# Attention of an image block: exact scores from fp32 operands in two row tiles instead of a three-part bf16 split

## What is computed

```python
qkv = jnp.einsum('bnc,oc->bno', xt, qkv_w)            # xt: (16, 1024, 192)
q, k, v = ...                                          # each (16, 6 heads, 1024, 32)
attn = jnp.einsum('bhnd,bhmd->bhnm', q, k) * SCALE
attn = jax.nn.softmax(attn, axis=-1)
out = jnp.einsum('bhnm,bhmd->bhnd', attn, v)
out = jnp.einsum('bnc,oc->bno', out, proj_w) + proj_b
```

## Time and profile before

| | us |
|---|---|
| median of 3 runs | 14572.99 (14550.2 to 14592.92) |
| the profiled execution | 14591.93 |
| its span | 14590.1 |

### The profile page before, as it was taken

The page is one execution under the profiler, slowest core; times in us unless marked ns, Lnnn a source line. Parts: engine busy times, 40 slices in busy tenths (PEclk is TensorE's granted clock), DMA queues, the critical chain, the costliest instruction groups (busy, mean ns, idle before and its releaser), DMA issues. The chain is left out here.

```text
span 14590.1 us, 88624 instructions
## 1 busy us (share of the span) xinstructions
PE 8678.6 (59%) x26672; PEld 2793.6 (19%) x26816; DVE 9257.5 (63%) x8214; ACT 4330.1 (30%) x4371; POOL 6262.8 (43%) x2937
## 2 busy tenths in 40 slices
PE   6474674746648466484664846648466384663846
PEld 1121221212212122121221312113122131221312
DVE  4756747567485674856748566575665756657566
ACT  2323233232322323223232232322323223232232
POOL 2715417154171541715417154261642716427164
PEclk8676766767667676676766767767676676766767
DMA  3505125051240512405124051340513405134051
GB/s 81 125 16 137 46 73 125 16 142 41 79 120 16 144 39 80 119 16 144 39 79 120 16 147 36 86 112 16 150 35 83 113 16 150 36 84 113 16 150 36
DMA packets 364229, 1164.38 MB, mean 80 GB/s; under 512 B 61487, under 2 KB 63039, under 8 KB 363599
## 3 DMA queue, kind: packets, MB, share of 16 engines
q1 hardware_dynamic: 358363, 1155.62, 31.0%
q10 hardware_dynamic: 3988, 1.01, 0.1%
q0 software_dynamic: 1248, 0.64, 0.0%
HBM read 959.86 MB, written 121.63 MB: 74 GB/s over the span
## 5 line engine op out<-in xcount | busy, mean ns | idle before, releaser
L796 PE MATMUL ps<-arena,sel_y 128*32 128x512 f32 x6144 | 2200.3, 882 | 4138.9 <-POOL arena L1037 4138.9
L1037 POOL TENSOR_TENSOR arena<-arena 128x1024 f32<-128x1024 f32 x1536 | 3798.8, 2474 | 635.2 <-DVE arena L986 597.6
L986 DVE TENSOR_TENSOR_SCAN arena<-ps,arena 128x1024 f32<-128x1024 f32 x1536 | 3514.6, 2290 | 717.2 <-POOL arena L1027 682.1
L902 ACT ACTIVATE ps<-arena,v_na 128x1024 f32<-128x1024 f32 x1536 | 1713.5, 1118 | 4085.7 <-DVE arena L986 3476.6
L796 PEld LDWEIGHTS ps<-arena,sel_y 128*32 128x32 f32 x6144 | 471.6, 150 | 5876.7 <-POOL arena L1037 3739.4
L617 DVE TENSOR_REDUCE arena<-ps 128x1 bf16<-128x1024 f32 x768 | 933.8, 1223 | 1015.6 <-PE ps L480 1015.0
L1027 POOL TENSOR_TENSOR arena<-arena 128x1024 f32<-128x1024 f32 x512 | 1201.3, 2346 | 468.7 <-DMA arena<-scan_dtu 468.7
L1019 POOL TENSOR_TENSOR arena<-arena,XN 128x1024 f32<-128x1024 f32 x32 | 75.2, 2350 | 2871.1 <-DVE arena L931 2871.1
L980 DVE TENSOR_TENSOR arena<-arena,ps 128x1024 f32<-128x1024 f32 x768 | 919.3, 1197 | 534.9 <-DMA arena<-scan_dtu 534.9
L597 ACT ACTIVATE arena<-ps 128x1024 f32<-128x1024 f32 x768 | 744.2, 1021 | 1056.4 <-PE ps L532 1056.4
L532 PE MATMUL ps<-arena 65*128 65x512 bf16 (+1 forms) x2928 | 759.3, 397 | 62.6 <-ACT arena L597 26.2
(11 more groups left out here) (213 smaller groups left out, 12246.7 us busy)
## 6 DMA issues: line engine op xcount, KB each, us to landing
arena<-scan_dt SPq DMA_DIRECT2D x768, 512.0 KB, 4.6
arena<-scan_dtu SPq DMA_DIRECT2D x768, 512.0 KB, 4.6
arena<-scan_bc SPq DMA_DIRECT2D x256, 512.0 KB, 6.3
arena<-arena SPq DMA_DIRECT2D x1152, 64.0 KB, 2.0
scan_dt<-arena SPq DMA_DIRECT2D x64, 512.0 KB, 9.8
scan_dtu<-arena SPq DMA_DIRECT2D x64, 512.0 KB, 7.6
scan_dt<-arena SPq DMA_DIRECT2D x64, 256.0 KB, 11.0
scan_dtu<-arena SPq DMA_DIRECT2D x64, 256.0 KB, 11.2
```

The source lines that it names most:

```text
L796: mm = nc.tensor.matmul(ps[3][32 * q:32 * q + 32, HALF * h:HALF * h + HALF], sel_y[:, r, :], hc[i % NHC][:, HALF * h:HALF * h + HALF], sta ...
L902: nc.scalar.activation(ps[1 + i % 2][:], dtr[:, i // 2 % RING, :], ACT.Exp, scale=v_na[:, at:at + 1]).then_inc(m_da, 1)
L986: nc.vector.tensor_tensor_scan(hs[:, i % 2, o], ps[1 + i % 2][:, o], bu[:, i % 2, o], 0.0, ALU.mult, ALU.add).then_inc(m_h, 1)
L1037: pool.tensor_tensor(hc[i % NHC], hs[:, i % 2, :], Cb[:, 2 * (k // 2) + f, :], ALU.mult).then_inc(m_hc, 1)
```

## The change

Queries and keys of a head stay fp32. Head h lies in tile h // 2 at row 64 * (h % 2), 32 rows, of `QQ` and `KK`; the weights `w_q` and `w_k` are laid out with zeros between (22 more weight loads before the image loop, in 32-column pieces). The row behind the 32 is 1 in the keys (a bias vector `v_one` on the copy from PSUM) and the negated maximum in the queries. The exact scores are one fp32 product of 33 rows per head and half. The rough scores read the upper two bytes of the same fp32 words as bf16, every second word. Six projections of 128 columns take the place of three; four of them follow rough scores 1, 3, 5 and 7, and the values follow rough scores 8 to 15. The split on ScalarE, VectorE and GpSimd, GpSimd's clearing of `KL`, the 72 transfers an image and PE's wait for them go.

```diff
-        w_qk = sb("w_qk", [128, 2, 3 * 128])
+        w_q = sb("w_q", [128, 2, 3, 128])
+        w_k = sb("w_k", [128, 2, 3, 128])
+        v_one = sb("v_one", [128, 1])
...
+            for h in range(HEADS):
+                t, e = h // 2, h % 2
+                for w, at in ((w_q, 0), (w_k, 128)) if h < 4 else ((w_q, 128), (w_k, 192)):
+                    two(w[:, :, t, 64 * e:64 * e + DH], wqk[:, at + DH * h:at + DH * h + DH])
...
+        QQ = area([3, L])
+        KK = area([3, L])
+        QR = QQ.bitcast(BF16).rearrange("p t (l f) -> p t l f", f=2)[:, :, :, 1]
+        KR = KK.bitcast(BF16).rearrange("p t (l f) -> p t l f", f=2)[:, :, :, 1]
...
-        def attn_sp(sp):
...
         def attn_pool(pool):
-            pool.memset(KL[2 * DH:REST, :, :], 1.0).then_inc(a_one, 1)
-            pool.wait_ge(a_one, 1)
             pool.memset(V[:, :, :, DH:64], 1.0).then_inc(a_one, 1)
-            for i in range(3):
-                pool.wait_ge(a_mi, i + 1)
-                pool.tensor_tensor(LO[:, i, :], RS[:, i, :], MI[:, i, :], ALU.subtract).then_inc(a_lo, 1)
...
-            def project(i, P):
+            def project(n):
+                t, k = n // 2, n % 2
+                if n == 2:
+                    pe.wait_ge(a_qkc, 1)
+                if n == 3:
+                    pe.wait_ge(a_kc, 1)
+                if n >= 4:
+                    pe.wait_ge(a_qkc, n - 2)
...
-                        mm = nc.tensor.matmul(P[:, HALF * h:HALF * h + HALF], w_qk[0:m, c, 128 * i:128 * i + 128],
+                        mm = nc.tensor.matmul(ps[k][:, HALF * h:HALF * h + HALF], (w_q, w_k)[k][0:m, c, t, :],
...
                 for m in range(2):
-                    mm = nc.tensor.matmul(P[:, HALF * m:HALF * m + HALF], q[:, Q * j:Q * j + Q],
-                                          k[:, HALF * m:HALF * m + HALF], start=True, stop=True)
+                    mm = nc.tensor.matmul(P[:, HALF * m:HALF * m + HALF], QR[r:r + DH, t, Q * j:Q * j + Q],
+                                          KR[r:r + DH, t, HALF * m:HALF * m + HALF], start=True, stop=True)
...
-            project(0, ps[0])
-            project(1, ps[1])
+            project(0)
+            project(1)
             for i in range(2 * NCH):
...
                 rough(i, ps[2 + i % 2])
-                if 2 <= i < 2 + NCH:
-                    values(i - 2)
+                if i % 2 == 1 and i < 8:
+                    project(2 + i // 2)
+                if i >= 8:
+                    values(i - 8)
             max_rows(0)
-            project(2, ps[2])
...
                 pe.wait_ge(a_rc, 2 * (t + 1))
-                pe.wait_ge(a_dm[t], 16 * COPIES)
...
-                                for q, k, n in ((QM, KM, MAIN), (QL, KL, REST)):
-                                    mm = nc.tensor.matmul(P, k[0:n, 2 * t + e, Q * j:Q * j + Q],
-                                                          q[0:n, 2 * t + e, HALF * m:HALF * m + HALF],
-                                                          start=(n == MAIN), stop=(n == REST))
+                                r = slice(64 * e, 64 * e + DH + 1)
+                                mm = nc.tensor.matmul(P, KK[r, t, Q * j:Q * j + Q], QQ[r, t, HALF * m:HALF * m + HALF],
+                                                      start=True, stop=True)
...
-            high(0)
-            high(1)
-            middle(0)
-            middle(1)
+            for n in (0, 2, 3, 4, 5):
+                act.wait_ge(a_qk, n + 1)
+                if n % 2 == 0:
+                    nc.scalar.activation(QQ[:, n // 2, :], ps[0][:], ACT.Copy).then_inc(a_qkc, 1)
+                else:
+                    nc.scalar.activation(KK[:, n // 2, :], ps[1][:], ACT.Identity, bias=v_one[:]).then_inc(a_qkc, 1)
...
-                    if t == 0 and j < 2:
-                        (high, middle)[j](2)
...
-            rest(0)
-            rest(1)
+            dve.wait_ge(a_qk, 2)
+            nc.vector.tensor_scalar(KK[:, 0, :], ps[1][:], v_one[:, 0:1], None, ALU.add).then_inc(a_kc, 1)
             maxima(0, True)
```

More of the change, by code:

```diff
@@ L183, in build @@
         s_we = sem("exponentials_ready")
+        s_z1 = sem("ones_column_cleared")
         s_wz = sem("low_rank_weights_cleared")
@@ L285, in _ @@
             def _(dve):
+                nc.vector.memset(w_q[:], 0.0)
+                nc.vector.memset(w_k[:], 0.0)
                 nc.vector.memset(w_dt[RP:XDW, :, :, :], 0.0).then_inc(s_wz, 1)
+                nc.vector.memset(v_one[:], 0.0).then_inc(s_z1, 1)
+                dve.wait_ge(s_z1, 1)
+                for e in range(2):
+                    nc.vector.memset(v_one[64 * e + DH:64 * e + DH + 1, :], 1.0).then_inc(s_w, 1)
                 dve.wait_ge(s_al, 16 * K)
@@ L402, in build @@
         a_rc = sem("attn_max_rows_copied")
[L403 to L406, removed]
+        a_kc = sem("attn_first_keys_copied")
         a_one = sem("attn_ones_set")
@@ L474, in rough @@
                 h, j = i // NCH, i % NCH
[L475 to L478, removed]
+                t, r = head_rows(h)
                 for m in range(2):
-                    mm = nc.tensor.matmul(P[:, HALF * m:HALF * m + HALF], q[:, Q * j:Q * j + Q],
-                                          k[:, HALF * m:HALF * m + HALF], start=True, stop=True)
+                    mm = nc.tensor.matmul(P[:, HALF * m:HALF * m + HALF], QR[r:r + DH, t, Q * j:Q * j + Q],
+                                          KR[r:r + DH, t, HALF * m:HALF * m + HALF], start=True, stop=True)
                 mm.then_inc(a_s, 1)
@@ L543, in attn_pe @@
                         pe.wait_ge(a_e, 2 * (NCH * t + j))
-                        if j == 1:
-                            pe.wait_ge(*((a_oc, t) if t > 0 else (a_rs, 3)))
+                        if j == 1 and t > 0:
+                            pe.wait_ge(a_oc, t)
                         for m in range(2):
@@ L607, in attn_dve @@
         def attn_dve(dve, b):
-            def rest(i):
-                dve.wait_ge(a_qkc, i + 1)
-                nc.vector.tensor_tensor(RS[:, i, :], ps[i][:], HI[:, i, :], ALU.subtract).then_inc(a_rs, 1)
             def maxima(t, both):
@@ L617, in maxima @@
                     nc.vector.reduce_max(MX[:, i:i + 1], P[:], AX.X).then_inc(a_m, 1)
-                    if i == 2 * NCH:
-                        rest(2)
                     if t == 2:
```

28 lines of the change are left out of this document (5 added, 23 removed).

## The result

The kernel after takes 15328.5 us (15299.2 to 15355.0), the kernel before 14568.8 (14550.2 to 14592.9): a ratio of 1.052, interval 1.049 to 1.055. The change made the kernel 5% slower. The forecast of 15105 had the sign; its own range (14990 to 15220) was too low, the wider one (14980 to 15560) holds the time, though only by the room left in it for rivals that did not come. The profiled execution took 15311.9, its span 15310.1, at a mean granted clock of 0.68 (0.70 before).

A forecast was written before the change was run, and what follows sets the result against it. PE was taken as the bound in everything touched; 23.2 + 2.1 + 1.2 + 3.0 + 0.7 + 1.5 = 31.7 us an image, x16 = 507, + 6 = 513 on 14591.9 gave 15105; own range 14990 to 15220, wider 14980 to 15560.

The forecast's parts named there:

- The bound and the prologue: First projection to first exact score: PE bounds it, six projections make 82.9 us against 59.8, +23.2 an image.
- The gift: Third projection: the early clock rise in four of sixteen images goes, +2.1 us an image on average.
- once-only weight loads: Before the image loop: twenty-two more weight loads over three queues, and two clears, +6 us once.
- Row tiles side by side: Exact scores: two heads' fp32 products run together, 1.87 us a step (+0.0); longer weight loads +1.2 an image.
- A: Exact scores: rival that row tiles do not run side by side, 44 us an image, 15815 us; chance 0.09.
- B: Exact scores: rival that tiles run partly side by side, 11 us an image, 15285 us; chance 0.10.
- Strided bf16: Rough scores: reading every second bf16 word of fp32 data costs nothing; upper bound a doubling.
- C: Rough scores: rival that strided reads run at half rate, 27 us an image, 15540 us; chance 0.08.
- D: Prologue: rival that the clock rises early, from the third projection on, 14460 to 14550 us; chance 0.05.
- Heads together, pair starts, last pair: Score loop: both heads finish together and wait for exponentials, +3.0 us an image at pair starts, +0.7 in the last pair.
- The clock in the loop: Score loop: the clock rises a step later in some images, +1.5 us an image, bounds 0 and 8.
- The copies, the split, GpSimd: Ahead of the exact scores: the 72 copies and GpSimd's subtractions are hidden, so removing them is worth nothing on the path.

The follow-up runs named there:

- e2: Kernel after with the second channel block of projections and values padded from 64 to 128 rows with zeros: 14768.0 us, 1.014 of before.
- e1: Kernel after with exact scores taking 64 rows of each operand instead of 33, the added rows zeros: 15010.6 us, 1.031 of before.
- e9: Kernel after with 72 unused 64 KB copies an image back on SyncE's queue, PE waiting for them before the second pair: 15330.1 us, 1.053 of before.
- e10: Kernel after with rough scores of 33 rows instead of 32: 15047.3 us, 1.031 of before.
- e5: Kernel after with projections and values padded to 128 rows and both exact and rough scores at 64 rows: 14306.8 us, 0.983 of before.
- e4: Kernel before with its three projections and its values padded to 128 rows: 14362.6 us, 0.986 of before.
- e6: Kernel after with projections and values padded to 128 rows, exact scores at 64, and head and half loops exchanged: 14416.4 us, 0.991 of before.

## Why the prediction was right in sign and low in size

**The bound and the prologue: right.** PE is the bound in both stretches. The sum gave 82.9 us for the new prologue; all sixteen are within 0.1 of 83.1. The parts agree too: 9.8 for a pair and a projection (9.81), 1.4 until rough score 0 (1.47), 2.2 bare for the guard (2.24).

**The gift: right.** No image after has the early rise of the earlier trace rows, and all prologues are equal. That is the 0.8 us by which the mean prologue grew beyond 23.2. For the once-only weight loads 6 us were put; the first projection starts 3.7 us later.

**Row tiles side by side: right, A and B fell.** 1.91 us for eight instructions and the changeover, where A needed 3.4 and B 2.3. For the rate the Trainium skill gives for four row tiles (TensorE: Matmul & The Clock Gate, Part 3, 3.07 of 4) no run here has a case; two tiles take 0.06 us a step more than the eight bf16 products of the earlier trace rows.

**Strided bf16: right, C fell.** A rough score takes 0.96 cold and 0.55 warm up to the next product, against 0.96 and 0.53 for packed operands. The Trainium skill (SBUF — State Buffer, the section on the DMA port swizzle) lets bf16 stride within a 16-byte line at full rate; the trace agrees for a step of two in both operands.

**D fell** for the kernel as changed: 0.50 through the whole prologue. With full projections (e2) the early clock does come, and the prologue takes 45.2 us where D had 55; D had put 16.0 us for the first two projections (10.3 in e2) and 4.5 for each other one (3.7 and one of 5.4). PE hardly rests in either kernel (42.45 of 46.60 us in e2's prologue); what differs is how many rows the products have, and with it the alternation between 128 and 64.

**Heads together, pair starts, last pair: about right.** The start of the second pair of heads (it read 5.0 in the earlier trace rows, and 5.9 was forecast):

```profile
1154.17 1.99 PE L514 MATMUL ps<-arena 33*128 33x512 f32 x8 [0.28 <-ACT arena L562]
1156.09 0.62 PE L463 MATMUL ps<-arena 32*128 32x512 bf16 x2
1156.25 1.94 ACT L572 ACTIVATE arena<-ps 128x1024 f32<-128x1024 f32 x2 [1.08 <-PE ps L514]
1157.33 2.90 PE L514 MATMUL ps<-arena 33*128 33x512 f32 x8 [0.61 <-ACT arena L572]
1160.15 0.97 PE L463 MATMUL ps<-arena 32*128 32x512 bf16 x2
```

1160.15 minus 1154.17 is 5.98. The second group stretches to 2.90 us at a granted clock of 1.00 because head 1's products wait for the second exponential, which ends at 1158.19, as the prediction had it (exponentials until 4.1, then 1.7). In the last pair steps alternate between 3.78 and 4.06 us (starts of the scores at 1235.82, 1239.60 and 1243.66), a mean of 3.92 against 3.71: 0.2 a step, where 0.1 was put.

**The clock in the loop: the step that failed.** The prediction read that the clock had risen within 12.8 us of the first score, noted that the new products have 33 rows rather than 128 and 65, and then priced this at 1.5 us an image, with 8 as the upper bound. The half clock went from 17.5 to 54.3 us an image. At e1's price of 0.42 that is 15.6 us (16.6 at the 0.45 that the images of the kernel after give). The prediction had 2.8 for it, the 1.5 and the loop's share of the gift (5.3 x 4/16 = 1.3). The other 5.8 us of the loop stand against 4.9. So the missing term is 15.6 - 2.8 = 12.8 us, x16 = 205, and 15105 + 205 = 15310 against 15311.9 of the profiled execution. That it fits so closely is luck: the loop's 0.9 us beyond 4.9, x16 = 14, and the slightly shorter rest of the images cancel. The bound of 8 had only a late first rise in it, and that rise came later than the bound had it, too: in the second image the clock stays up only from 31.8 us after the first score, against 12.8 before. That the clock would also fall again, in the second and third pair, was weighed under rival A alone, as something that thin products might do, and it does not need A. The wider range holds the time only because it had room for B (15285) and C (15540); neither happened, and that B's number lies near the measured time is luck.

**The copies, the split, GpSimd: worth nothing, right.** e9 shows it for the transfers. No run puts the split back; that the prologue came out as its sum, which has nothing for it, is what speaks for it.

**Open.** Why the clock answers to the rows of the products rather than to PE's busy time isn't settled beyond that zeros count. e1 shows the rows alone for the loop; for the projections rows and the alternation between 128 and 64 changed together (e2). e10 shows that what may overlap acts as well, and in its loop overlap and clock are not separated. Whether rows of data other than zeros would do more wasn't tried. Nor was the scheme of the kernel before with full projections and rough scores of 64 rows, so whether e5 beats the best form of the older scheme is open; it beats e4 by 56 us.

## What to carry to other kernels

Before costing a change by instruction counts, read at which granted clock each group runs, and ask whether the change makes the products of that stretch thinner in rows; the price of that here (15.6 us an image) was larger than that of all edits to the loop together (5.8). Where rows are free, padding them with zeros took no time on PE at an equal clock (eight score instructions last 1.99 us with 33 rows and with 64) and gave back the clock (a projection from 8.08 to 3.60 us). And products that need the same number of rows of the array, in different halves of it, ran beside each other even when they were unrelated (e5, e10). A bound on a clock term has to hold a clock that falls again, not only one that rises late.

## What the runs showed of the hardware

The clock stayed at 1.2 GHz through 83 us in which PE was busy 96% of the time (79.42 of 83.09 us) with fp32 products of 128 and 64 rows in turn and bf16 products of 32; with 128 rows in all projections, the added ones zeros, it rose within the first (e2). In the loop zeros in rows 33 to 63 cut the time at 1.2 GHz from 54.3 to 10.5 us an image (e1). The clock also fell with PE having waited only twice for 0.26 us (at 1115.9 in the kernel after). A product of 33 rows in place of 32 changed what may run beside it (e10: 281 us). And the order of two tiles' products in the stream made no difference (e6: 1.93 us for eight either way).
